# Writing the tanh of an LSTM cell into PSUM instead of SBUF, in a recurrence of 256 steps

## The reference

```python
def step(carry, xs):
    h, c = carry
    xi_t, xf_t, xg_t, xo_t = xs
    i_t = jax.nn.sigmoid(xi_t + h @ V_i)
    f_t = jax.nn.sigmoid(xf_t + h @ V_f)
    g_t = jnp.tanh(xg_t + h @ V_c)
    o_t = jax.nn.sigmoid(xo_t + h @ V_o)
    c_new = h * c + i_t * g_t
    h_new = o_t * jnp.tanh(c_new)
    return ((h_new, c_new), h_new)
```

## Time and profile before

| | |
|---|---|
| Median of 3 runs | 995.34 us (995.21 to 996.75) |
| Profiled execution, its own time | 994.94 us |
| Its span, first to last instruction | 993.1 us |
| Busy over the span: PE, PEld | 770.1 us (78%), 571.4 us (58%) |
| Busy: DVE, ACT, POOL | 557.3, 556.9, 369.8 us |
| The 256 executions of L713 | 43.8 us busy, 171 ns mean |
| The 256 executions of L1061 | 40.7 us busy, 159 ns mean |
| TensorE's granted clock, mean over the span | 0.745 |

### The profile page before, as it was taken

One profiled execution on the slowest core, in us unless ns is written; L12 is line 12 of the kernel. 1 busy time (PEld: TensorE's weight loads), 2 busy tenths in 40 slices (PEclk: granted clock), 3 DMA queues, 4 the chain that ended last, 5 costly groups with the idle time before them and its releaser, 6 DMA issues.

```text
span 993.1 us, 18107 instructions
## 1 busy us (share of the span) xinstructions
PE 770.1 (78%) x6224; PEld 571.4 (58%) x6224; DVE 557.3 (56%) x1560; ACT 556.9 (56%) x1580; POOL 369.8 (37%) x296
## 2 busy tenths in 40 slices
PE   5799976666666666666666557999869999899996
PEld 2477865555554555555555444788736666466663
DVE  3798753555445355333333336887556776567675
ACT  2667743333355355333333335677558888688884
POOL 0777720000000000000000006877348888588885
PEclk7999995555555555555555558999969999899999
DMA  9600000000001100000000000000000010100001
GB/s 222 161 2 1 2 1 1 1 1 1 1 1 75 75 1 0 1 1 1 1 0 1 1 0 1 2 1 3 1 0 2 2 76 2 77 2 1 1 2 22
DMA packets 5861, 18.54 MB, mean 19 GB/s; under 512 B 1093, under 2 KB 2822, under 8 KB 5254
## 3 DMA queue, kind: packets, MB, share of 16 engines
q1 hardware_dynamic: 5478, 17.21, 6.0%
q10 hardware_dynamic: 288, 0.13, 0.1%
HBM read 9.47 MB, written 0.52 MB: 10 GB/s over the span
## 4 chain that ended last, share of the span: by engine, by line
PE 35%; POOL 21%; DVE 15%; ACT 13%; issue 12%; DVEq 1%; SPq 1%; DMA 1%; POOLq 1%; ACTq 0%
POOL zw L813 20%; PE bank L458 10%; DVE bank L1055 6%; PE bank L460 6%; PE bank L332 5%; ACT scan_io L709 5%; PE bank L349 5%; ACT tcell L713 5%; PE bank L297 4%; DVE hr L1061 4%; DVE hid L888 1%; PE bank L319 1%; DVE dist L873 1%; PE bank L362 1%; PE bank L277 1%
## 5 line engine op out<-in xcount | busy, mean ns | idle before, releaser
L773 POOL TENSOR_TENSOR st<-tent,tentx 128x768 f32<-128x768 f32 x96 | 150.9, 1606 | 524.7 <-DVE tentx L881 511.5
L813 POOL TENSOR_TENSOR zw<-hid,zw 128x512 f16<-128x512 f32 x176 | 204.1, 1160 | 49.0 <-ACT zw L740 30.3
L458 PE MATMUL bank<-hr,lv 64*64 64x8 f32 x512 | 96.8, 261 | 158.8 <-DVE hr L1061 158.8
L458 PEld LDWEIGHTS bank<-hr,lv 64*64 64x64 f32 x512 | 72.5, 200 | 205.4 <-DVE hr L1061 205.3
L1160 DVE SCALAR_TENSOR_TENSOR hid<-bank,wsc,st 128x512 f32<-128x512 f32 x176 | 132.0, 750 | 75.6 <-ACT st L744 70.2
L709 ACT ACTIVATE scan_io<-bank 64x16 f32<-64x16 f32 x256 | 49.3, 193 | 210.7 <-PE bank L460 210.5
L1055 DVE TENSOR_TENSOR_SCAN bank<-scan_io 64x32 f32<-64x32 f32 x256 | 57.5, 225 | 163.2 <-ACT scan_io L709 163.2
L498 PE MATMUL bank<-st,wh 128*128 128x512 f16 x352 | 136.8, 389 | 11.5 <-POOL st L806 5.4
L744 ACT ACTIVATE st<-bank,wsc 128x512 f32<-128x512 f32 x176 | 121.0, 688 | 35.3 <-PE bank L499 17.6
L499 PE MATMUL bank<-st,wl 128*128 128x512 f16 x352 | 136.7, 388 | 0.0
L513 PEld LDWEIGHTS bank<-w2p,zw 128*128 128x128 f16 x1408 | 96.9, 98 | 45.3 <-POOL zw L813 4.0
(11 more groups left out here) (149 smaller groups left out, 1133.5 us busy)
## 6 DMA issues: line engine op xcount, KB each, us to landing
w13s<-w SPq DMA_DIRECT2D x8, 704.0 KB, 18.0
w2f<-w SPq DMA_DIRECT2D x4, 384.0 KB, 26.8
w13s<-wh SPq DMA_DIRECT2D x2, 704.0 KB, 3.4
w13s<-wl SPq DMA_DIRECT2D x2, 704.0 KB, 4.6
wh<-w13s SPq DMA_DIRECT2D x2, 704.0 KB, 3.9
wl<-w13s SPq DMA_DIRECT2D x2, 704.0 KB, 5.2
w2f<-w2p SPq DMA_DIRECT2D x2, 384.0 KB, 5.2
w2p<-w2f SPq DMA_DIRECT2D x2, 384.0 KB, 5.8
```

The costliest lines, as they stand in the source:

```text
L458: nc.tensor.matmul(both[:, 0, t, :], lv[:, C:2 * C], prev, start=False, stop=True, skip_group_check=True)
L773: nc.gpsimd.tensor_tensor(st[p][:, t, k:k + KG, :].rearrange("p k (y x) -> p k y x", x=16), ty, tx, ALU.mult)\
L813: nc.gpsimd.tensor_tensor(hl[:, u % MR, :], hid[:, u % MR, :], hh[:, u % MR, :], ALU.subtract)\
```

## The change

`tcell` is no longer a tensor of its own in SBUF, but the first 8 columns of bank 6 in PSUM, on the same 64 partitions. L713 writes it there and L1061 reads it from there. No instruction, wait or order changes on any engine, and no other line does:

```diff
@@ -122,7 +122,7 @@
         hr = sb("hr", [C, 2 * W, B])
         scan_io = sb("scan_io", [C, 2, B, 4])
         cell = bank[7][0:C, 0:B * 4].rearrange("p (b k) -> p b k", k=4)
-        tcell = sb("tcell", [C, B])
+        tcell = bank[6][0:C, 0:B]
         tog = sb("tog", [C, B])
         hup = sb("hup", [P, 2, BQ, W])
         rw = sb("rw", [P, 2 * E])
```

## The result

The changed kernel takes 987.7 us (median of 6 runs, 986.26 to 990.02), the one before 996.05 us in the runs beside it (994.56 to 999.28): ratio 0.9915, 95% interval 0.9893 to 0.9936, or 8.35 us less. The forecast was 985.9 us, 9.5 us less than before. The profiled execution has a span of 986.9 us, against 993.1 before.

What follows compares the result with a forecast made beforehand. The recurrence was taken as bound by latency, one short instruction after another. (-38 + 1) ns x 256 = -9.5 us from 994.94 gave 985.5, plus 0.40 for the median of runs: 985.9 us, range 982.8 to 996.8.

Steps and rivals of the forecast that it cites:

- The path: In the recurrence, whatever L713 saves or loses the step does too; a step falls from 1.66 to 1.62 to 1.63 us.
- The ScalarE write: L713's write to PSUM instead of SBUF was to be 38 ns shorter, 171 to about 133 ns.
- the way out should cost about the same more: At L713, ScalarE's 38 ns difference between reading SBUF and PSUM was assumed to hold for writing too.
- the two bounds: L713's write saving: 0 by VectorE's memsets at one end, -38 ns by ScalarE's reads at the other, -46 for the range.
- VectorE shows no difference in either direction: VectorE was taken to read and write PSUM and SBUF alike: reads 160 against 159 ns, memsets both 85 ns.
- each engine is symmetric: Each engine's SBUF-PSUM difference was taken as alike for reading and writing, supporting -38 ns for L713's write.
- The VectorE read: L1061's second input in PSUM was to cost +1 ns per step, from L1065's 160 against 159 ns.
- The start of L1061: The 0.10 us between L713's end and L1061's start was to stay unchanged, with +0.02 us as upper bound.
- Rival 1: L713's write costs the same in both memories, leaving only +1 ns per step: +0.3 us, 995.6 us; chance 0.23.
- rival 2: VectorE pays more for L1061's PSUM operand than ScalarE gives back: +5.1 us, 1000.5 us; chance 0.13.
- The sum: Over the recurrence's 256 steps, (-38 + 1) ns x 256 = -9.5 us, forecasting 985.9 us, 1.0% less.
- What hides what: Gap-filling work in the recurrence (L431, L687, L1026) was to stay off the path with a step 0.04 us shorter.

Runs made afterwards that it cites:

- Experiment 1: Kernel before the change, with the tanh of gate o (L711) written to PSUM in place of the cell's tanh; 995.26 us beside 995.22.
- Experiments 3, 4 and 7: 3 and 4: kernel before with the cell moved from PSUM to SBUF, tcell in SBUF (1003.88 us) or PSUM (993.89 us); experiment 7 has its own line.
- experiment 7: Kernel before plus unused extra ScalarE and VectorE instructions in the last 45 steps, each waiting for its predecessor's end on its engine; 993.87 us.
- experiment 9: Changed kernel with only the two waits before L1061 written in the opposite order; 967.8 us.
- experiment 8: Changed kernel with the two waits before L1055 and before L1061 written in the opposite order; 951.54 us, ratio 0.9559 to the kernel before.
- experiment 5: Kernel before plus unused extra ScalarE and VectorE instructions in the last 45 steps, with SBUF or PSUM operands and no added waits or semaphore updates; 996.84 us.

## Why the prediction was right, and where its sizes were off

- **The path.** Right. The stage is one serial chain, and what L713 and L1061 saved (24 + 4 ns) the step saved (29 ns; the median step fell from 1.667 to 1.638 us, less than the forecast's 1.62 to 1.63). Experiment 1 shows the counterpart: the same 24 ns at L711, which is not on the path, gave nothing.
- **The ScalarE write, -38 ns.** The sign was right, the size was not: 24 ns. The step that failed is "the way out should cost about the same more". Experiments 3, 4 and 7 show that this is about true of an instruction whose other side is in SBUF (destination 35 or 36 ns, source 37 at 8 columns in experiment 7: 208 and 171). L713's source was already in PSUM, and there the second move is worth only 24. The price was taken from a pair of rows in which the other operand was in SBUF. Why the two moves don't add up stays open. The 24 lies between the two bounds, but the upper one, 0, came from a memset on VectorE, and no row of ScalarE spoke for it. The other end, 46, used L575's mean of 201 ns, which mixes 199 ns of overlapping executions with 206 of waiting ones; by the latter it is 202 - (206 - 45) = 41 ns.
- **"VectorE shows no difference in either direction".** Wrong in small: writing PSUM costs it 8 or 9 ns (the scan 225 against 217, the extra instruction 167 against 158), which memsets don't show. So "each engine is symmetric" fails for VectorE, which gains on one side and loses on the other. ScalarE is nearly symmetric: 35 ns for the destination and 37 for the source with the other side in SBUF, 24 and 26 with it in PSUM (experiment 7).
- **The VectorE read, +1 ns.** It was -4. The comparison of L1065 with L1061 was not one of memories alone: L1065 writes and reads every fourth element, and with both inputs in SBUF it takes 167 ns, so its 160 already held a saving of 7. That the strides make up the rest was not tried. Experiment 1 adds that only the second input counts. Both inputs in PSUM were not tried.
- **The start of L1061, 0 with a bound of +0.02 us.** Right: 0.10 us before and after, and 0.032 where one wait is carried (experiment 9). L1160's 0.12 us is not from a PSUM operand: the separate wait ahead of it (L1159, whose target is computed in a loop) is a piece of 40 ns on VectorE's sequencer, where L1060 is one of 21 ns, and the 19 ns between them make up the difference.
- **Rival 1** (no saving) fell with L713's 147 ns, **rival 2** (VectorE pays more) with L1061's 155 ns and its unchanged start. The page of the Trainium skill "Perfetto Trace Analysis", section "Optimizing Scalar/DVE Operations", points the right way for ScalarE (51 against 93 ns, a difference of 42, where 24 to 44 ns were measured), but its 125 against 60 ns for VectorE does not show in these runs: an input in PSUM costs 0 to 7 ns less, an output 8 or 9 ns more.
- **The sum.** By the measured terms the forecast would have been (-24 - 4) x 256 = -7.2 us. The stage gave 7.4 in the profiled execution, and the medians 8.35, with an interval of 6.4 to 10.7 (996.05 times 0.0064 and 0.0107). The forecast of 9.5 lies in it, but with one term too large by 14 ns and one off by 5 the other way, which together leave 9 ns a step, 2.3 us, too much. That the two errors lay on opposite sides, and that the medians gave 1 us more than the stage, is luck. The remainder between 7.4 and 8.35 is within what single executions differ by.
- **What hides what.** Right but for one step of 255. There the matmuls L431 started late and held up L458; that step took 1.86 us before, after the change and in experiment 8, so it gained nothing. In the others no filling work came onto the path, not even with the step at 1.50 us.
- **What was not seen.** The prediction used the 0.10 us between ScalarE and VectorE only to look for a cost of PSUM. The rows showed 0.03 us where VectorE or ScalarE waits once, for a result of VectorE, and the difference of 0.07 us, twice per step, was worth 36 us, four times the change itself.

## What to carry to other kernels

In a serial chain of small instructions the fixed time of each link is what counts: a small ScalarE result that VectorE alone reads belongs in PSUM, where it ends 24 ns earlier if its source is in PSUM and 35 if it is in SBUF, from 8 to 256 columns, but only a link that is on the path and waits for its predecessor pays it back. Where an instruction has two waits, look at which of them the instruction carries: the one that is over last should be that one (0.032 us against 0.10 here). Price a move between memories from rows whose other operands lie where yours do, since the two sides don't add up.

## What the runs showed of the hardware beyond what was expected

- ScalarE's tanh of 8 columns, when it starts after its predecessor's end: SBUF to SBUF 208 ns, SBUF to PSUM 173, PSUM to SBUF 171, PSUM to PSUM 147. With 256 columns it is 416, 381, 378 and 353. Reading and writing the same bank in one instruction costs nothing more (147 ns in bank 7 and in bank 6).
- The recorded duration of an instruction depends on what ran before it: the same PSUM to SBUF tanh of 8 columns takes 171 ns when it waits for its predecessor's end and 158 when it starts within it, PSUM to PSUM 147 and 159. Durations of overlapping instructions can't be compared with those of a chain. On VectorE the overlap took 6 to 8 ns off each form of 8 columns, and the destination still showed (152 ns to SBUF and 160 to PSUM in experiment 5).
- VectorE's scalar_tensor_tensor of 8 columns takes 158 ns from SBUF, 158 with the first and 155 with the second input in PSUM, and 167 with a PSUM output, each behind its predecessor's end.
- A separate wait that is over last costs 0.07 us between ScalarE and VectorE (0.101 against 0.032 us), though the sequencer's piece in the chain is only 0.02 us long. One that is over early costs nothing: L1061 still has two waits in experiment 8 and starts 0.032 us behind L713.
